# A one-core conv-attention and mixture-of-experts block: VectorE's norm of the next batch behind the query taps, and the last 36 expert outputs added by GpSimd

## The reference, cut to what matters

```
xn = _ln_c(x)                                   # norm over the 96 channels of a pixel
value, query = dwconv3x3(xn), dwconv3x3(xn)     # depthwise, stride 1
key, off     = dwconv3x3(xn, 2), dwconv3x3(xn, 2)
pos = tanh(gelu(norm(off)) @ w_off2 + ref)      # 784 sampling points of a batch
vs  = bilinear sample of value at pos
x = x + w_out @ (query @ key^T * SCALE @ vs)    # linear attention, 12 heads
t = norm over the channels of x                 # 3136 tokens x 96
masked = top-2 of softmax(t @ gate_w + gate_b), renormalised   # 4 experts
for e in experts:                               # 96 -> 384 -> 96
    x += masked[e] * (gelu(t @ w1[e] + b1[e]) @ w2[e] + b2[e])
```

## Time and profile before

| | us |
|---|---|
| median of 3 runs (805.04 to 811.27) | 805.53 |
| the profiled execution | 807.02 |
| its span, first to last instruction | 805.2 |
| PE busy | 727.1 |
| DVE busy | 577.4 |
| ACT busy | 384.7 |
| POOL busy | 200.3 |

### The profile page before, as it was taken

The page is one execution under the profiler, slowest core; times in us unless marked ns, Lnnn a source line. Parts: engine busy times, 40 slices in busy tenths (PEclk is TensorE's granted clock), DMA queues, the critical chain, the costliest instruction groups (busy, mean ns, idle before and its releaser), DMA issues.

```text
span 805.2 us, 9619 instructions
## 1 busy us (share of the span) xinstructions
PE 727.1 (90%) x3186; PEld 509.7 (63%) x3186; DVE 577.4 (72%) x1511; ACT 384.7 (48%) x722; POOL 200.3 (25%) x184
## 2 busy tenths in 40 slices
PE   5898998789999998789999998999989999999970
PEld 5657565556676665456766565666646666888860
DVE  5688738689989657799895577999933464666640
ACT  2323115534565415525654237445423276999960
POOL 4003500011139610011197101111573011111111
PEclk9996999889999998869999999999989999999995
DMA  8007100034564420036644412336454133544443
GB/s 185 6 0 199 42 0 1 12 88 93 99 180 87 99 44 9 12 87 149 168 96 98 81 27 52 75 75 163 106 114 95 21 79 71 106 87 98 81 85 52
DMA packets 33729, 64.86 MB, mean 81 GB/s; under 512 B 6800, under 2 KB 24208, under 8 KB 33392
## 3 DMA queue, kind: packets, MB, share of 16 engines
q0 software_dynamic: 15616, 24.10, 20.1%
q1 hardware_dynamic: 14336, 32.59, 14.2%
q10 hardware_dynamic: 3728, 7.55, 3.1%
HBM read 30.30 MB, written 14.65 MB: 56 GB/s over the span
## 4 chain that ended last, share of the span: by engine, by line
PE 52%; DMA 25%; DVE 9%; issue 6%; POOL 4%; ACT 4%; ACTq 0%; POOLq 0%; DVEq 0%
DMA xbuf<-ye 22%; PE py L733 13%; PE pd L649 8%; PE ph L565 6%; PE ph L749 4%; PE ph L750 3%; PE ph L751 3%; PE pa L516 3%; POOL big L1447 3%; PE pa L637 3%; PE pd L619 2%; PE pd L498 1%; DVE val L1116 1%; PE pa L629 1%; DMA big<-value_table,rows 1%
## 5 line engine op out<-in xcount | busy, mean ns | idle before, releaser
L733 PE MATMUL py<-hid,w 128*96 128x448 f32 x504 | 239.9, 558 | 21.9 <-DVE ye L1395 12.9
L989 ACT ACTIVATE hid<-ph,b 128x448 f32<-128x448 f32 x252 | 158.9, 632 | 174.6 <-PE ph L751 168.2
L1456 POOL DMA_DIRECT2D xbuf<-ye x112 | 93.3, 833 | 508.4 <-DMA xbuf<-ye 247.2
L749 PE MATMUL ph<-x_hi,w_hi 96*128 96x448 f32 x252 | 169.2, 671 | 0.0
L1447 POOL DMA_INDIRECT big<-value_table,rows x64 | 98.6, 1541 | 83.8 <-DVE rows L1176 57.1
L733 PEld LDWEIGHTS py<-hid,w 128*96 128x96 f32 x504 | 83.5, 168 | 41.2 <-ACT hid L989 13.9
L1395 DVE SCALAR_TENSOR_TENSOR ye<-py,b,gate_all 96x448 f32<-96x448 f32 x112 | 75.5, 676 | 30.3 <-PE py L733 18.6
L750 PE MATMUL ph<-x_lo,w_hi 96*128 96x448 f32 x252 | 95.1, 377 | 0.0
L751 PE MATMUL ph<-x_hi,w_lo 96*128 96x448 f32 x252 | 94.4, 375 | 0.0
L1116 DVE SCALAR_TENSOR_TENSOR query<-xpad,conv_w,query 128x784 f32<-128x784 f32 x80 | 78.3, 1026 | 0.5
L1116 DVE SCALAR_TENSOR_TENSOR val<-xpad,conv_w,val 128x784 f32<-128x784 f32 x80 | 78.3, 1026 | 0.4
(11 more groups left out here) (164 smaller groups left out, 1065.2 us busy)
## 6 DMA issues: line engine op xcount, KB each, us to landing
gate_all<-gate_rows SPq DMA_DIRECT2D x56, 336.0 KB
xbuf<-ye POOLq DMA_DIRECT2D x112, 168.0 KB
value_table<-valT ACTq DMA_DIRECT2D x6, 1176.0 KB, 8.8
out<-xbuf SPq DMA_DIRECT2D x28, 168.0 KB, 2.0
xbuf<-in_x SPq DMA_DIRECT2D x3, 1176.0 KB, 10.8
value_table<-valT SPq DMA_DIRECT2D x2, 672.0 KB, 5.4
big<-value_table,rows POOLq DMA_INDIRECT x64
value_table<-valT SPq DMA_DIRECT2D x2, 504.0 KB, 6.8
```

The source lines that it names most:

```text
L733: nc.tensor.matmul(py[e % 2][0:C, 0:GPIX], w2[:, c, :], hid[:, k % 3, :], start=(j == 0), stop=(j == CPE - 1)).then_inc(hid_used, 1)
L749: nc.tensor.matmul(bank, w1_hi[:, cols], xh(b, g), start=True, stop=False)
L989: nc.scalar.activation(hid[:, k % 3, :], ph[k % 2][:, 0:GPIX], ACT.Gelu, bias=b1[:, k % NCH:k % NCH + 1]).then_inc(hid_act, 1)
L1456: pool.dma_start(x_of(b)[:, g * GPIX:(g + 1) * GPIX], ye[0:C, e, :], accum_op=ALU.add).then_inc(ye_summed, 16)
```

## The change

It does three things.

1. In VectorE's `rest(b)`, `norm_x(b + 1)` stands behind the query taps 2 to 8 instead of in front of them (batches 1 and 2; batch 0 and batch 3 have no such step there).
2. Of the 112 adds of outputs, the last 36 (numbers 76 to 111: the last eight of batch 2 and all 28 of batch 3) are no DMAs but `tensor_tensor` adds of 96x448 on GpSimd itself, counted by a new semaphore `ye_added`. VectorE's wait for a free `ye` buffer and SyncE's wait before a store use it for those (`after_sums`).
3. The four tables have new numbers.

`last_experts` is also written with chunk numbers over all batches; `EARLY_CHUNKS` is 252 in both kernels, and so each instruction there works on the same data as before.

```diff
+EARLY_CHUNKS = 252
+ALL_CHUNKS = BATCH * CHUNKS
+BY_DMA = 76
...
 CHUNKS_AHEAD = [
...
-    dict(valT=(42, 42, 43, 43, 44, 44, 45), xT=(45, 46, 46, 47, 47, 48, 48), keyT=(49, 49),
+    dict(valT=(40, 40, 41, 41, 42, 42, 43), xT=(43, 44, 44, 45, 45, 46, 46), keyT=(47, 47),
-         pad=(54, 54, 71, 72, 72, 73), kv=(73, 73, 79, 79), mix=(79, 79, 80, 80), y=(80, 80, 80, 80, 80, 80, 80, 80),
+         pad=(67, 67, 68, 68, 69, 69), kv=(69, 69, 70, 70), mix=(70, 70, 71, 71), y=(71, 71, 71, 71, 71, 71, 71, 71),
...
 SUMS_AHEAD = [(0, 0, 0, 0, 0, 0, 0, 0),
-              (15, 16, 17, 18, 19, 20, 21, 21),
-              (38, 39, 40, 41, 42, 43, 44, 45),
-              (66, 67, 68, 69, 69, 70, 71, 72)]
+              (14, 15, 16, 16, 17, 17, 18, 18),
+              (36, 37, 38, 38, 39, 39, 40, 40),
+              (63, 64, 65, 66, 66, 67, 67, 68)]
...
+        def after_sums(eng, n):
+            if n <= BY_DMA:
+                wait(eng, ye_summed, 16 * n)
+            else:
+                eng.wait_ge(ye_added, n - BY_DMA)
...
             def store_result(b, g):
-                sp.wait_ge(ye_summed, 16 * (b * OUTPUTS + EXPERTS * (g + 1)))
+                after_sums(sp, b * OUTPUTS + EXPERTS * (g + 1))
...
                     key_tap(k)
                 turn()
+                for k in range(QUERY_AHEAD, TAPS):
+                    turn()
+                    query_tap(b, k)
                 if with_head:
                     turn()
                     norm_x(b + 1, turn)
-                for k in range(QUERY_AHEAD, TAPS):
-                    turn()
-                    query_tap(b, k)
                 turn()
                 sample(b, turn)
...
-                        wait(dve, ye_summed, 16 * (n + 1 - EXPERTS))
+                        after_sums(dve, n + 1 - EXPERTS)
...
                     pool.wait_ge(ye_ready, FREE_OUTPUTS + n + 1)
-                    wait(pool, ye_summed, 16 * n)
-                    pool.dma_start(x_of(b)[:, g * GPIX:(g + 1) * GPIX], ye[0:C, e, :], accum_op=ALU.add).then_inc(ye_summed, 16)
+                    after_sums(pool, n)
+                    to = x_of(b)[:, g * GPIX:(g + 1) * GPIX]
+                    if n < BY_DMA:
+                        pool.dma_start(to, ye[0:C, e, :], accum_op=ALU.add).then_inc(ye_summed, 16)
+                    else:
+                        p.tensor_tensor(to, to, ye[0:C, e, :], ALU.add).then_inc(ye_added, 1)
```

More of the change, by code:

```diff
@@ L775, in second_product @@
                 def second_product(k):
[L776 to L777 removed]
+                    c, n, m = k % NCH, k // CPE, k - EARLY_CHUNKS
+                    e, j = n % EXPERTS, k % CPE
                     if j == 0:
[L780 removed]
+                        pe.wait_ge(ye_ready, FREE_OUTPUTS + n - 1)
                     bank = py[e % 2][0:C, 0:GPIX]
[L782 removed]
+                    pe.wait_ge(hid_hi_ready, m + 1)
                     nc.tensor.matmul(bank, w2_hi[:, c, :], hid_hi[:, k % 3, :], start=(j == 0), stop=False)
                     nc.tensor.matmul(bank, w2_lo[:, c, :], hid_hi[:, k % 3, :], start=False, stop=False)
[L785 to L786 removed]
+                    pe.wait_ge(hid_lo_ready, m + 1)
+                    nc.tensor.matmul(bank, w2_hi[:, c, :], hid_lo[:, m % 2, :], start=False, stop=(j == CPE - 1)).then_inc(hid_used, 1)
                 pe.wait_ge(w2_split, 1)
[L789 to L791 removed]
+                first_product(EARLY_CHUNKS)
+                first_product(EARLY_CHUNKS + 1)
+                for k in range(EARLY_CHUNKS + 2, ALL_CHUNKS):
                     first_product(k)
                     second_product(k - 2)
[L794 to L795 removed]
+                second_product(ALL_CHUNKS - 2)
+                second_product(ALL_CHUNKS - 1)
             pe.wait_ge(ident_in, 16)
@@ L991, in experts, with last_experts @@
                 return gelus_to
-            def last_experts(b):
-                for k in range(CHUNKS):
-                    act.wait_ge(hid_full, b * CHUNKS + k + 1)
+            def last_experts():
+                for k in range(EARLY_CHUNKS, ALL_CHUNKS):
+                    act.wait_ge(hid_full, k + 1)
                     for dst, ready in ((hid_hi, hid_hi_ready), (hid, hid_act)):
@@ L1414, in split_w2, with last_experts @@
                 v.tensor_tensor(w2_lo[:, :, :], w2[:, :, :], w2_hi[:, :, :].bitcast(f32), ALU.subtract).then_inc(w2_split, 1)
-            def last_experts(b, outputs_to):
-                for k in range(CHUNKS):
-                    dve.wait_ge(hid_act, b * CHUNKS + k + 1)
-                    wait(dve, hid_used, b * CHUNKS + k - 1)
-                    v.tensor_tensor(hid_lo[:, k % 2, :], hid[:, k % 3, :], hid_hi[:, k % 3, :].bitcast(f32), ALU.subtract).then_inc(hid_lo_ready, 1)
-                    if k >= CPE + 1 and (k - 1) % CPE == 0:
-                        outputs_to(b * OUTPUTS + (k - 1) // CPE)
+            def last_experts(outputs_to):
+                for k in range(EARLY_CHUNKS, ALL_CHUNKS):
+                    m = k - EARLY_CHUNKS
+                    dve.wait_ge(hid_act, k + 1)
+                    wait(dve, hid_used, k - 1)
+                    v.tensor_tensor(hid_lo[:, m % 2, :], hid[:, k % 3, :], hid_hi[:, k % 3, :].bitcast(f32), ALU.subtract).then_inc(hid_lo_ready, 1)
+                    if m >= CPE + 1 and (m - 1) % CPE == 0:
+                        outputs_to((k - 1) // CPE)
                 outputs_to(BATCH * OUTPUTS)
```

66 lines of the change are left out of this document (27 added, 39 removed), and 24 rows, old and new, of the table OUTPUTS_AHEAD.

## The result

The changed kernel takes 778.09 us (median of 4 runs, 776.23 to 779.96) against 805.28 (805.03 to 811.27) for the kernel before. The ratio, of the means of these runs, is 0.9645, 95% interval [0.9594, 0.9696]. The forecast was 773, with 762 to 788. The profiled execution took 776.23 us, its span is 774.4, so 30.8 us of span are gone. Lines of the changed kernel are 8 to 13 higher than those of before.

The account below looks back on a forecast made before the run. TensorE is busy 727 of 805 us, so a change can win where it idles or runs below full clock. 807.0 - 15.2 - 6.0 - 13 + 1 = 773.8, 1.5 less by the median, said as 773; range 762 to 788.

Parts of the forecast that it names:

- the case it called likeliest: Whole kernel: the forecast itself, 773 us, with its own range 766 to 781 and chance 0.62.
- (a) The end: Behind TensorE's last matmul: the queue of accumulating DMAs, 21.2 us, becomes output, add and store, 6.0; gain 15.2.
- (b) The stop in the last phase: Last 84 chunks: VectorE no longer waits for a `ye` buffer, so TensorE keeps 1.22 us per chunk; gain 6.0.
- (c) Order and tables: Batches 1 to 3: earlier gathers, kv and gates from moved norm and new tables; gain 13, as 8 plus 5.
- The short wait at the second kv pair: Batch 1: TensorE arrives at 268.8, sampled values allow kv at 271.5; a new wait of 2.7 us.
- the prediction's sign for it: Between 310 and 675 us of the trace: TensorE idles some 10 us less.
- upper end: Order and tables, batches 1 to 3: at most 30 us, 12.3 + 12.9 idle and about 5 for low clock.
- (d) The collision: GpSimd's adds beside VectorE's work: a new collision, put at a loss of 1 us.
- third rival: Last phase: adds and `hid_lo` exclude each other, TensorE waits; mild 776 to 796, chance 0.08; hard some 840, 0.02.
- The first rival: Whole kernel: only the end is won, gathers no earlier; 782 to 799, mostly 787 us; chance 0.20.
- The second: Whole kernel: all bubbles go, gates covered and gathers done before kv; 759 us, range 756 to 765; chance 0.08.
- two rules: VectorE instructions with two SBUF inputs: don't stall descriptor generation; exclude SBUF-reading GpSimd instructions for the whole instruction.

Follow-up runs that it names:

- e2_order_only: The changed kernel with all adds as DMAs (BY_DMA = 112), so only order and tables differ from the kernel before; 796.74 us.
- e4_taps_one_input: The kernel before, with query taps 2 to 8 beside experts taking their second operand from PSUM instead of SBUF, which omits the tap sum; 796.39 us, one run.
- after_again: The changed kernel run again with no edit; 778.80 us.
- e7_adds_twice: The changed kernel with each of the last 36 adds issued twice on GpSimd, which alters the result; 786.16 us.
- e1_adds_only: The kernel before with only the last 36 adds moved to GpSimd, order and tables as before; 791.75 us.
- e3b_norm_in_front_by_time: The changed kernel with the norm back in front of the query taps and the output numbers shifted to keep their times, batches 1 and 2; 794.14 us.
- e5_all_gpsimd: The changed kernel with all 112 adds on GpSimd and none by DMA (BY_DMA = 0); 810.75 us.

## Why the prediction was right, and where it was not

The forecast of 773 is 5.1 us below the median, inside its range, and the case it called likeliest is the one that came. Of the 5.1 us, 2.4 are the terms below (773.8 by the profile, 776.2 measured). The rest comes from the executions that were profiled: the forecast took 0.8 off, as that of before lay above its median, and that of the changed kernel lies 1.9 below its own.

**(a) The end: 15.2 predicted, 14.0 measured.** The add was well sized (1.0 taken, 1.12 measured). Mis-sized was "from the start of the last store to the span's end is 3.9 us and stays": it is 5.3. The 3.9 was read rightly (the store of before is issued at 801.31); that it "stays" was wrong. It is 3.9 in the three profiled kernels whose last add is a DMA (before, e2_order_only, e4_taps_one_input) and 5.2 to 5.5 in all those whose last add is GpSimd's. The store itself lands 2.0 us after its issue in both kernels; what grew is the time behind the landing, from 1.9 to 3.3 us, in which the trace shows no instruction. Why that hangs on the kind of the adds stays open.

**(b) The stop in the last phase: 6.0 predicted, 4.7 measured.** The beat is 1.22 us and nothing stops, as predicted. Mis-sized were the phase's ends. The prediction allowed 0.8 us for the filling of the pipeline; the phase takes 104.6 - 84 x 1.22 = 2.1 more than its beat, at its start (the first chunks come at 662.59, 663.55 and 664.96) and at its end (the last matmul waits 0.28 and takes 0.45).

**(c) Order and tables: 13 predicted, 12.1 measured** by the first pair of profiles, 8.0 with after_again's start of the last phase, 8.7 to 13.0 by medians. Batch 1 went step by step as written: last gather 8.7 us earlier (7 taken), kv at 271.02 (271.5 predicted), past chunk 91 at 342.49 (342.2 predicted); and batches 2 and 3 gave 12.06 - 7.55 = 4.5 (5 taken, as an estimate). The norm that now comes later left little uncovered: TensorE waits 1.25 us for `xT` at 413.38 in batch 2, where the prediction feared 13 in all.

Two steps behind these numbers were wrong all the same. The short wait at the second kv pair did not show: the transposes stand in front of it and TensorE was there at 271.0, not 268.8. And the sentence "PE's work is the same, so only its idle time can change" does not hold, as the prediction's sign for it did not come: from 310 to the last phase idle time fell from 25.1 to 19.8 us, by 5.3 and not by 10 (the stages above and the earlier trace rows). TensorE alone, from the span's start to the first matmul of the last phase, of before and of after, which is the same set of matmuls:

```profile
0.00:674.65 674.65, 621.68 (x2682) 420.32 (x2683) 507.64 (x1398) 287.65 (x554) 177.57 (x155) 0.95 0.36 79
```

```profile
0.00:662.59 662.59, 613.10 (x2682) 413.43 (x2683) 506.78 (x1398) 287.46 (x554) 169.56 (x155) 0.96 0.35 80
```

Of the 12.06 us, 3.5 are idle time (53.0 to 49.5) and 8.6 are busy time of the same matmuls. With after_again (617.14 busy, 49.49 idle) it is 3.5 and 4.5. The prediction had named the low clock as part of an upper end only, so that 3.5 and 8.6 add up to nearly its 13 is in part luck.

A stop can be paid twice, as a wait and in the matmuls behind it. The stop in the last phase of before shows it: TensorE ran at a granted clock of 1.00 before it and at 0.50 behind it, the lower of its two levels (1.2 GHz where full clock is 2.4).

```profile
772.42:775.41 2.99, 0.00 (x1) 0.01 (x1) 1.27 (x3) 0.78 (x2) 0.79 (x1) 0.99 0.11 23
775.41:778.40 2.99, 2.99 (x8) 2.53 (x9) 1.54 (x3) 1.15 (x2) 0.00 (x1) 0.50 0.44 58
```

At batch 1's gates in the changed kernel the clock is low already ahead of the wait, behind the small matmuls of the offsets (96x2), and stays low through it; there the two matmuls at 342.49 take 1.78 us that take 0.92 at full clock.

```profile
336.00:337.65 1.65, 1.65 (x6) 1.00 (x5) 1.65 (x3) 0.00 (x0) 0.00 (x0) 0.51 1.01 267
337.65:342.49 4.84, 0.01 (x1) 0.03 (x1) 4.80 (x9) 0.74 (x2) 0.00 (x0) 0.50 0.22 70
```

**(d) The collision: 1 predicted, 0 measured.** The third rival's mechanism is real, and its condition was put right: it costs from the point where the slack of 0.82 us between `hid_lo` and its matmul is used up. In its price the prediction let a `hid_lo` wait for a whole add; here the two start 0.08 us apart with `hid_lo` first, so the add waits 0.44 and the next `hid_lo` only 0.28. e7_adds_twice shows the price past the slack, 0.16 us per output for one more add.

**The first rival** (gathers no earlier) is refuted by the trace, and its reason by e4_taps_one_input; the kernels without the new order came 5 to 7 us above its 787 (e1_adds_only 791.75, e3b_norm_in_front_by_time 794.14). **The second** failed as written: the tables run to chunk 91 and a wait of 4.84 us is left.

On the two rules. SBUF — State Buffer of the Trainium skill (section Who interferes with whom) infers that an instruction with two SBUF inputs does not stall descriptor generation. The prediction applied this to the gathers, and there it fails: e4_taps_one_input shows the two-input taps to be the cause (1.0 us for 2.7). But the gathers are not plain descriptor generation: their issue takes its row numbers from the tile `rows` in SBUF. The plain DMAs that GpSimd issues beside the same taps are not slowed, in the kernel before:

```profile
257.58 2.92 DVE L1116 SCALAR_TENSOR_TENSOR query<-xpad,conv_w,query 128x784 f32<-128x784 f32 x3
...
257.90 0.99 POOL L1456 DMA_DIRECT2D xbuf<-ye  x1
```

Seventeen of them start inside a row of taps with at least 0.9 us of it to go; they take 0.79 to 0.99 us, median 0.79, as elsewhere. The 20 gathers that start so take 2.3 on average. So the inference agrees with the plain DMAs. The same section's other rule, that a two-input instruction and a GpSimd instruction that reads SBUF keep each other out for their whole length, agrees with e5_all_gpsimd and e7_adds_twice; it would cover the gathers too if their issue reads `rows` in that way, which no run here separates.

The cut at 76 adds thus has its reason: the first seven of GpSimd's adds, ahead of the last phase, take 1.14 us, the other 29 meet only `hid_lo`; earlier ones would meet taps.

## What to carry to other kernels

Before an elementwise step is put on GpSimd, look at what VectorE runs at that moment: an add of 1.12 us took 1.84 on average and cost VectorE 0.6 where it met taps and other instructions with two SBUF inputs, and 36 of the same adds won 14 to 19 us where VectorE had slack. A table of positions counted in turns belongs to one order of steps; reorder the steps and it must be laid out again by time, or the test of the order measures the table. In judging a bubble, count its idle time and the slower matmuls around it: over the whole stretch busy time fell by more (4.5 to 8.6 us) than idle time (3.5).
